# Edge counting: the one-hot of the sources of each set's fourth tile moves from the Vector engine to the Pool engine

## The reference, cut to what matters

```python
e  = einsum('ehd,ehd->eh', k[src], q[dst]) / 8
ex = exp(e - segment_max(e, dst)[dst])
attn = ex / segment_sum(ex, dst)[dst]
a  = segment_sum(attn[:, :, None] * v[src], dst)
```

## Time and profile before

| | us |
|---|---|
| median of 3 runs | 1819.24 |
| lowest and highest run | 1818.44, 1821.59 |
| the profiled execution, its own time | 1823.7 |
| span of the profiled execution | 1822.1 |
| PE, DVE, ACT, POOL busy in the span | 1602.7, 998.7, 733.0, 560.9 |

### The profile page before, as it was taken

How to read it: one execution, slowest core, us unless ns; L and a number is a source line. 1 busy time by engine, 2 the same in 40 slices (tenths; PEclk the granted TensorE clock), 3 DMA queues, 4 the chain that set the end, 5 groups by cost and what they waited for, 6 DMA issues and landing times. The chain is left out here.

```text
span 1822.1 us, 31339 instructions
## 1 busy us (share of the span) xinstructions
PE 1602.7 (88%) x9860; PEld 1171.6 (64%) x9860; DVE 998.7 (55%) x1981; ACT 733.0 (40%) x1641; POOL 560.9 (31%) x638
## 2 busy tenths in 40 slices
PE   3998757899979896999999999569999999898994
PEld 2555534788868564559999999455555555645662
DVE  8533379788856576530000000469999999431233
ACT  2232345666646234442222221255555555422331
POOL 6777700111100221440000000335555554233133
PEclk7999979899989997999999999779999999998997
DMA  7538710788662302557665550465555554639985
GB/s 206 118 92 265 255 44 7 187 244 236 152 169 58 90 1 100 193 175 293 229 230 211 205 204 9 124 172 170 156 156 155 156 155 120 220 77 284 350 266 180
DMA packets 146054, 305.94 MB, mean 168 GB/s; under 512 B 42492, under 2 KB 59744, under 8 KB 141220
## 3 DMA queue, kind: packets, MB, share of 16 engines
q1 hardware_dynamic: 106590, 224.70, 39.4%
q0 software_dynamic: 39360, 79.86, 15.6%
HBM read 226.47 MB, written 77.96 MB: 167 GB/s over the span
## 5 line engine op out<-in xcount | busy, mean ns | idle before, releaser
L2198 PE MATMUL acc<-prod,ohy 128*64 128x256 f32 x1056 | 248.8, 386 | 8.5 <-DVE prod L2316 8.5
L2242 ACT ACTIVATE ohy<-oh,RECS 128x64 f32<-128x64 f32 x704 | 187.2, 337 | 152.3 <-PE acc L2198 152.2
L2198 PEld LDWEIGHTS acc<-prod,ohy 128*64 128x64 f32 x1056 | 138.4, 138 | 132.9 <-issue 71.5
L2175 POOL DMA_INDIRECT rows<-up_dram,idx x176 | 167.3, 951 | 143.4 <-DVE prod L2316 101.7
L1952 DVE TENSOR_SCALAR FT<-y_ps,b2T 128x188 f32<-128x188 f32 x32 | 13.2, 413 | 323.5 <-PE y_ps L1901 323.5
L321 POOL DMA_INDIRECT rec_dram<-recs,pos x157 | 162.1, 1032 | 60.8 <-issue 49.6
L2201 PE MATMUL acc<-prod,ohy 128*64 128x256 f32 x704 | 177.4, 395 | 0.0
L1889 PE MATMUL hid_ps<-FT,W 128*128 128x188 f32 x1024 | 167.8, 325 | 0.7 <-ACT FT L1926 0.7
L2316 DVE TENSOR_TENSOR prod<-w_ps,rows 128x768 f32<-128x768 f32 x176 | 166.3, 945 | 0.0
L1889 PEld LDWEIGHTS hid_ps<-FT,W 128*128 128x128 f32 x1024 | 165.3, 192 | 0.9 <-issue 0.9
L1901 PE MATMUL y_ps<-hid,W 128*128 128x188 f32 x1024 | 164.5, 323 | 0.0
(11 more groups left out here) (401 smaller groups left out, 2912.4 us busy)
## 6 DMA issues: line engine op xcount, KB each, us to landing
W<-in_L_ffn_w SPq DMA_DIRECT2D x16, 4096.0 KB, 16.4
raw_dram<-X SPq DMA_DIRECT2D x40, 585.9 KB
X<-raw_dram SPq DMA_DIRECT2D x40, 585.9 KB
bankW_sp<-in_L_ffn_W_sp SPq DMA_DIRECT2D x2, 4096.0 KB, 23.2
h_dram<-h3e SPq DMA_DIRECT2D x22, 256.0 KB, 4.3
h<-h_dram SPq DMA_DIRECT2D x22, 256.0 KB
QF<-q_dram SPq DMA_DIRECT2D x20, 250.0 KB, 6.0
b2B<-in_L_ffn_b_sp SPq DMA_DIRECT2D x17, 256.0 KB, 8.4
```

The costliest lines, as they stand in the source:

```text
L2175: pool.indirect_dma_start(out=rows[:, t, :], out_offset=None, in_=up_dram, in_offset=bass.IndirectOffsetOnAxis(ap=idx[:, par, t:t + 1], ax ...
L2198: upper = lambda m: nc.tensor.matmul(acc[0:HALFB, bank, :].rearrange("p (b c) -> p b c", c=MUL)[:, m:4:3 - m, :], ohs[:, 1 + m, :], pr[:, ...
L2242: last = nc.scalar.activation(ohy[:, t % OHY, i, :], oh[:, par, t, :], ACT.Copy, scale=RECS[:, bass.ds(BATCH * g + t, 1), 4 + i])
```

## The change

The last of the four `ohS` instructions of each set is taken from DVE and given to POOL, in the same layout. POOL's loop over the sets is now written out, and for each set it grants the region, then waits for the keys (`keyed`, a new semaphore, signalled at L782) and for `counted` of the set three before, makes the one-hot, and signals `hot_by_pool`, also new. PE waits for this semaphore ahead of the set's fourth tile. The split of the first queries stays behind the loop on POOL's queue.

```diff
-                (granted,) = sems_in(st)("region_granted")
+                granted, keyed, hot_by_pool = sems_in(st)("region_granted", "keys_made", "last_one_hots_ready")
...
-                        groups(pool, grant)
+                        def last_one_hot(g):
+                            slot = SET * (g % AHEAD) + SET - 1
+                            pool.wait_ge(keyed, 1 if g < AHEAD * EARLY_ROUNDS else 2)
+                            pool.wait_ge(counted, SET * g + SET)
+                            nc.gpsimd.tensor_scalar(ohS[:, slot, :], nodes16[:], RECS[:, SET * g + SET - 1, 0:1], None, ALU.is_equal
+                                                    ).then_inc(hot_by_pool, 1)
+
+                        pool.wait_ge(numbered, 1)
+                        for g in range(SETS):
+                            grant(g, g % AHEAD)
+                            last_one_hot(g)
                         split(pool, 0, 0)
...
-                            nc.vector.tensor_copy(RECS[:, mine, 0], srcI[:, mine])
+                            nc.vector.tensor_copy(RECS[:, mine, 0], srcI[:, mine]).then_inc(keyed, 1)
...
-                            for t in range(SET):
+                            for t in range(SET - 1):
                                 last = nc.vector.tensor_scalar(ohS[:, SET * k + t, :], nodes16[:], RECS[:, n + t, 0:1],
                                                                None, ALU.is_equal)
                             last.then_inc(hot, 1)
...
                             pe.wait_ge(hot, g + 1)
                             for t in range(SET):
+                                if t == SET - 1:
+                                    pe.wait_ge(hot_by_pool, g + 1)
                                 slot = (SET * g + t) % CRING
```

## The result

The changed kernel takes 1845.3 us (median of 4 runs, 1842.57 to 1846.71), the kernel before 1820.41 in the same comparison: a ratio of 1.0127, with a 95% interval from 1.0103 to 1.0150. That is +24.9 us. The sign is as forecast and the time lies in the range, but +11.5 was forecast. The profiled executions stand at 1845.02 and 1823.7, which is +21.3.

What follows compares the result with a forecast made beforehand. DVE was taken to bound the counting. A net loss of 0.225 us in each of 44 sets (+9.9) and the moved split (+1.6) made +11.5 us, so a median of 1830.7 us; range 1822 to 1857.

Steps and rivals of the forecast that it cites:

- What bounds the kernel: In the counting stage DVE, busy 39.90 of 40 us, sets the pace; PE needs 1.27 of 1.51 us a set.
- What the change removes: One of DVE's four `ohS` a set, 0.295 us, leaving 1.215 us; at most 13.0 us won over 44 sets.
- What POOL's instruction takes: POOL's one-hot of 626 elements in each set takes 0.74 us, with ends of 0.67 and 1.32.
- Rival C: POOL spends two steps on an element of its one-hot: 1.32 us, hold 1.12, time 1857.3 us; chance 0.18.
- What it costs DVE: POOL's one-hot holds DVE 0.52 us a set against 0.295 saved: a loss of 0.225, +9.9 us over 44 sets.
- length less 0.22: In the counting, each POOL instruction holds DVE for its own length less 0.22 us.
- rival D: POOL becomes the counting's bound: grant, one-hot and up to 0.885 us of waiting, 2.155 a set, time 1849.2; chance 0.14.
- The new waits: PE's wait for `hot_by_pool` and POOL's for `counted` cost nothing, hidden by POOL's lead of more than a set.
- The split and the clock: The queries' split moves into DVE's last two sets, where PE falls to half clock: +1.6 us; elsewhere the clock holds.

## Why the prediction was right in sign and wrong in size

- **What bounds the kernel**: right. DVE set the pace, and what it lost moved everything behind it.
- **What the change removes**: 1.215 us for DVE's own work was right; 1.21 is measured where POOL does next to nothing. That 13.0 us could be won was wrong: PE's own pace of 1.39, and not its busy time of 1.27, stands behind it.
- **What POOL's instruction takes: this is the step that failed.** It was put at 0.74 us, with ends of 0.67 and 1.32; it is 1.87. The slope of a CAST was carried to a TENSOR_SCALAR because both read one tensor. The row that seemed to support it was an AFFINE_SELECT of 128 elements, another instruction; a TENSOR_SCALAR of 128 takes 0.60, not 0.28. The Trainium skill, page "GPSIMD Engine Reference", section "Performance pitfalls for Q7 kernels", puts a price on a body that compares and selects. In the runs here it isn't the comparison that costs: an add takes the same 1.87. Rival C doubted this step, but its 1.32 was too short as well.
- **What it costs DVE**: the rule "length less 0.22" came from a CAST and a TENSOR_TENSOR and doesn't hold for this instruction, which held DVE for 0.67 to 0.93 us of its 1.9. The two errors worked against each other: the rule with the right length would have given (1.87 - 0.22 - 0.295) x 44 = +59.6. That the time lies in the range is luck. The Trainium skill, page "SBUF — State Buffer", section "Who interferes with whom", has the ports locked for a whole instruction. Here DVE got an `ohS` through in the middle of POOL's, and the measurement decides.
- **The bound that replaced it**: the sum was made as DVE's work and a hold. In fact POOL, back to back, became the bound. That was rival D's mechanism, but not for its reasons: the grants don't add to POOL's time, since the next one-hot starts when the last one ends, and it lasts some 0.25 us longer than by itself in the first rhythm and hardly at all in the second, where 0.885 of waiting was assumed. Its 1849.2 is near the measured time because an overpriced wait and grant stood in for an underpriced instruction.
- **The new waits**: right. Neither DVE's wait for `granted` nor PE's for POOL's one-hot appears among the waits of the stage; PE waits for DVE's `ohS`, 42 times. The lead that was to cover them was smaller than forecast, though: POOL starts a set's one-hot 0.12 us ahead of that set's `ohD` in the first rhythm (257.46 and 257.58) and 1.23 in the second (318.60 and 319.83), and not more than a set.
- **The split and the clock**: the place and the fall of the clock were right; the cost was 0.9 and not 1.6 us, since only one set ran at half clock and not two. In the stage itself the clock held as forecast but for one fall behind the second part of the keys: it was 0.57 on the mean of 272 to 276 us, after PE had been busy for 1.27 of the 4 us before. In the kernel before it did not fall there.

## What to carry to other kernels

Before work goes to a second engine, time that very instruction there by itself: type and width don't make a CAST a guide to a TENSOR_SCALAR. Then compare three paces, not two: the helper's own length, the first engine's rest with what the helper holds of it, and the engine that comes next. Where two engines are both "busy" all the time, take work from each of them in turn; the distance between two starts tells which one sets the pace.

## What the hardware showed that I had not expected

- A TENSOR_SCALAR on POOL costs about 2.5 ns an element (1.87 us for 626), whichever of the operations and types tried here it has, and a copy of the same row 0.70.
- That instruction holds DVE's `ohS` in two stretches, of up to about half a microsecond each, and lets one pass in between. Why it does is not settled.
- An unbroken stream of `ohS` on DVE kept a POOL instruction waiting until the stream ended: 37.07 us in place of 1.08. The POOL instruction before it had got into the same stream, so the stream alone does not explain it. In the counting, where an `ohD` comes every few instructions, POOL always got in; that the `ohD` is what lets it in was not tried.
- The two engines can settle into different rhythms, 2.14 or 1.88 us a set, by the phase in which they start.
